# Alternating narrow and wide query tiles in a top-k attention, and a verdict sent by DMA instead of TensorE

## What is computed

```python
draft = einsum('bhqd,bhkd->bhqk', qr, kr) + causal          # rotary q and k
num_remain = max(min(Sq, 128), Sq - int(Sq * 0.9))          # 204 of 2048
_, idx = top_k(draft, num_remain)                           # all others masked
attn = softmax(einsum('bhqd,bhkd->bhqk', qr, kr) / sqrt(HD) + mask)
out = einsum('bhqk,bhkd->bhqd', attn, v) @ Wo.T
```

## Time and profile before

| | us |
|---|---|
| median of 3 runs | 4733.16 |
| lowest, highest | 4732.83, 4733.44 |
| the profiled execution, its own time | 4739.29 |
| its span | 4737.5 |
| busy in the span: PE, DVE, ACT, POOL | 3524.3, 3173.2, 2688.0, 2023.6 |

### The profile page before, as it was taken

How to read it: one execution, slowest core, us unless ns; L and a number is a source line. 1 busy time by engine, 2 the same in 40 slices (tenths; PEclk the granted TensorE clock), 3 DMA queues, 4 the chain that set the end, 5 groups by cost and what they waited for, 6 DMA issues and landing times. The chain is left out here.

```text
span 4737.5 us, 56552 instructions
## 1 busy us (share of the span) xinstructions
PE 3524.3 (74%) x16248; PEld 1649.4 (35%) x16248; DVE 3173.2 (67%) x6104; ACT 2688.0 (57%) x4577; POOL 2023.6 (43%) x5916
## 2 busy tenths in 40 slices
PE   5777775677868757787885678888567888857776
PEld 2333332233323323333332233333233333324443
DVE  2444444688988758888884888887488888822222
ACT  0111111688858757886885688887478888820000
POOL 1121211655535755554575554456565445620000
PEclk8777776688989878898997789989779999978887
DMA  2111111100001010000100100010010000011111
GB/s 97 42 52 43 51 40 44 34 11 11 9 6 21 16 30 12 11 9 7 21 16 19 24 11 9 9 21 14 19 26 11 9 9 11 15 72 53 54 40 40
DMA packets 221534, 124.04 MB, mean 26 GB/s; under 512 B 187940, under 2 KB 206628, under 8 KB 221092
## 3 DMA queue, kind: packets, MB, share of 16 engines
q1 hardware_dynamic: 221092, 119.36, 8.9%
HBM read 76.28 MB, written 42.99 MB: 25 GB/s over the span
## 5 line engine op out<-in xcount | busy, mean ns | idle before, releaser
L868 PE MATMUL banks<-pT,v_sb 128*65 128x512 f32 x2176 | 1186.3, 629 | 34.9 <-ACT oT L972 33.4
L957 ACT ACTIVATE pT<-banks 128x512 f32<-128x512 f32 x1088 | 637.7, 592 | 641.3 <-PE banks L840 634.9
L816 PE MATMUL banks<-k_sb,q_sb 128*128 128x512 bf16 (+3 forms) x1280 | 515.5, 403 | 388.5 <-DVE sc L1121 355.0
L1144 DVE MAX8 near<-keys 128x8 f32<-128x256 f32 (+14 forms) x480 | 653.4, 1361 | 16.5
L948 ACT ACTIVATE junk<-sc,t_all 128x256 fp8e4<-128x256 f32 (+14 forms) x480 | 599.2, 1249 | 31.9 <-DVE sc L1121 30.1
L948 ACT ACTIVATE junk<-sc,tiny 128x256 fp8e4<-128x256 f32 (+14 forms) x480 | 595.5, 1246 | 36.5 <-DVE sc L1129 36.2
L948 ACT ACTIVATE junk<-sc,tt 128x256 fp8e4<-128x256 f32 (+14 forms) x480 | 598.4, 1247 | 1.4 <-POOL tt L1013 0.8
L834 PE MATMUL banks<-q_sb,k_sb 128*128 128x512 bf16 x1088 | 447.0, 411 | 146.4 <-DVE fb L1298 124.7
L1121 DVE TENSOR_SCALAR_CACHE_REDUCE sc<-banks 128x1024 f32<-128x1024 f32 (+7 forms) x512 | 501.3, 980 | 52.1 <-PE banks L821 30.0
L1129 DVE TENSOR_SCALAR sc<-sc,tt 128x256 f32<-128x256 f32 (+14 forms) x480 | 360.5, 814 | 241.6 <-POOL tt L1034 241.5
L818 PE MATMUL banks<-k_sb,q_sb 96*128 96x512 bf16 (+3 forms) x1280 | 504.8, 404 | 0.0
(11 more groups left out here) (247 smaller groups left out, 5469.8 us busy)
## 6 DMA issues: line engine op xcount, KB each, us to landing
q_sb<-scratch_qk SPq DMA_DIRECT2D x896, 32.0 KB, 1.9
scratch_qk<-parts SPq DMA_DIRECT2D x16, 960.0 KB, 3.7
a_x<-in_x SPq DMA_DIRECT2D x16, 512.0 KB, 3.2
scratch_x<-a_x SPq DMA_DIRECT2D x16, 512.0 KB, 2.6
scratch_attn<-o_sb SPq DMA_DIRECT2D x128, 64.0 KB, 1.6
c_xn<-scratch_attn SPq DMA_DIRECT2D x16, 512.0 KB, 3.6
c_x<-scratch_x SPq DMA_DIRECT2D x16, 512.0 KB, 4.5
out<-c_x SPq DMA_DIRECT2D x16, 512.0 KB, 2.6
```

Of the source, the lines that this page charges most:

```text
L816: nc.tensor.matmul(r_slot(n)[:, j:j + wj], q_sb[:, p % QS, 0, h, :], k_sb[:, group[p] % 2, 0, col:col + wj], start=True, stop=False)
L868: nc.tensor.matmul(psum[0:VP, 6, :], v_sb[:, group[p] % 2, kb, :], pT[:, n % PTS, :], start=(kb == 0), stop=(kb == blocks[p] - 1)).then_in ...
L957: nc.scalar.activation(pT[:, tn % PTS, :], psum[:, 4 + n % 2, :], ACT.Exp, scale=SCALE)\
L1144: v.max(near[:, h, :], z).then_inc(sm["key"], 1)
```

## The change

First, the order of places. Within each group of heads the tiles now come as 0, 15, 1, 14, 2, 13, and so on to 7, 8. A narrow tile always stands beside a wide one, and the two tiles of a pair have 17 blocks together.

Second, the verdict. PE's `flags` and its wait for `bad` are gone, and so is the wait of `turn_back` for `flg`. Instead SP waits for `bad` and issues a transfer of it (128 rows of 4 bf16 numbers) into one partition, `verdict`; DVE waits for its landing and reads 512 numbers with one instruction. `bad` and `verdict` alternate between two buffers by the count of searched places. The list of small instructions in `fall_back` now finds the head from `verdict` on one partition.

```diff
-PLACE = [(g, i) for g in range(HKV) for i in (range(TILES) if g % 2 == 0 else range(TILES - 1, -1, -1))]
+PLACE = [(g, i) for g in range(HKV) for n in range(TILES // 2) for i in (n, TILES - 1 - n)]
...
+                def carry_verdict(p):
+                    sp.wait_ge(sm["bad"], chosen[p + 1])
+                    if p >= 2:
+                        sp.wait_ge(sm["go"], p - 1)
+                    sp.dma_start(verdict[0:1, chosen[p] % 2, :, :], bad[:, chosen[p] % 2, :]).then_inc(carried[chosen[p] % 2], 16)
+
...
                 for j in range(N + 2):
+                    if searching(j):
+                        carry_verdict(j)
                     if j >= 2:
                         store(j - 2)
...
-                    if chosen[min(p + 2, N)]:
-                        pe.wait_ge(sm["flg"], chosen[min(p + 2, N)])
...
-                def flags(p):
-                    pe.wait_ge(sm["bad"], chosen[p + 1])
-                    if p >= 2:
-                        pe.wait_ge(sm["norm"], p - 1)
-                    nc.tensor.matmul(psum[:, 7, FLAGS:FLAGS + REP], b.ones16[:, :], bad[:, p % 2, :],
-                                     start=True, stop=True).then_inc(sm["flagged"], 1)
...
-                    gp.tensor_tensor(bad[:, p % 2, :], c, far, ALU.add).then_inc(sm["bad"], 1)
+                    if chosen[p] >= 2:
+                        pool.wait_ge(carried[chosen[p] % 2], 16 * (chosen[p] // 2))
+                    gp.tensor_tensor(bad[:, chosen[p] % 2, :], c, far, ALU.add).then_inc(sm["bad"], 1)
...
-                    dve.wait_ge(sm["flagged"], chosen[p + 1])
-                    v.tensor_scalar(heads_bad[:, :], psum[:, 7, FLAGS:FLAGS + REP], 0.0, None, ALU.add, ALU.max,
-                                    accum_out=flg[:, 0:1]).then_inc(sm["flg"], 1)
+                    dve.wait_ge(carried[chosen[p] % 2], 16 * (chosen[p] // 2 + 1))
+                    if chosen[p]:
+                        dve.wait_ge(sm["flg"], chosen[p])
+                    v.tensor_scalar(passed[:, :], verdict[:, chosen[p] % 2, :, :].rearrange("o q h -> o (q h)"), 0.0, None,
+                                    ALU.add, ALU.max, accum_out=flg[0:1, 0:1]).then_inc(sm["flg"], 1)
```

More of the change, by code:

```diff
@@ L632 @@
 R_AT = (0.06, 0.25, 0.42)
-FLAG_AT, NEXT_R_AT = 1.0, 0.75
+NEXT_R_AT = 0.75
 def phase_b(nc, b, dram):
@@ L716, in phase_b @@
         heads_bad = sb("heads_bad", [P, REP])
+        verdict = sb("verdict", [1, 2, P, REP], BF16)
+        passed = sb("passed", [1, P * REP], BF16)
         rec = sb("rec", [P, REP])
@@ L728, in phase_b @@
         psum = b.psum
-        sm = semaphores(nc, ctx, "fill rs evac sign t1 t2 df sel key dk bad flagged flg mask go st ex pv ot otr norm mf "
+        sm = semaphores(nc, ctx, "fill rs evac sign t1 t2 df sel key dk bad flg mask go st ex pv ot otr norm mf "
                         "vchain pchain", "b")
@@ L735, in phase_b @@
         written = [ctx.enter_context(nc.semaphore(f"b_written{n}")) for n in range(2)]
+        carried = [ctx.enter_context(nc.semaphore(f"b_carried{n}")) for n in range(2)]
         def r_slot(n):
@@ L901, in _ @@
                     seen, back = 0, not here(j - 2)
-                    held = None
                     for n in range(len(todo) + 1):
                         for kind, p, h in at[n]:
[L905 to L910, removed]
+                            scores(p, h)
                         if n == len(todo):
@@ L1174, in fall_back @@
                         dve.drain()
[L1175 to L1179, removed]
+                        then(v.tensor_reduce(heads_bad[0:1, :], verdict[:, chosen[p] % 2, :, :].rearrange("o q h -> o h q"),
+                                             AX.X, ALU.max))
+                        then(v.tensor_scalar(heads_bad[0:1, :], heads_bad[0:1, :], 0.0, None, ALU.is_gt))
+                        then(v.tensor_reduce(several[0:1, :], heads_bad[0:1, :], AX.X, ALU.add))
+                        then(v.tensor_tensor(heads_bad[0:1, :], heads_bad[0:1, :], b.steps[0:1, 0:REP], ALU.mult))
+                        then(v.tensor_reduce(c[0:1, :], heads_bad[0:1, :], AX.X, ALU.max))
+                        then(v.tensor_scalar(which[0:1, :], c[0:1, :], 0.5, None, ALU.subtract))
                         hb = dve.value_load(fbi[0:1, 7:8], min_val=0, max_val=REP - 1)
@@ L1218, in fall_back @@
                         then(v.tensor_reduce(c[0:QUAD, :], quads[0:QUAD, :], AX.X, ALU.max))
-                        then(v.tensor_scalar(several, several, 1.5, None, ALU.is_gt))
-                        then(v.tensor_tensor(c[0:QUAD, :], c[0:QUAD, :], several[0:QUAD, :], ALU.max))
+                        then(v.tensor_scalar(several[0:1, :], several[0:1, :], 1.5, None, ALU.is_gt))
+                        then(v.tensor_tensor(c[0:1, :], c[0:1, :], several[0:1, :], ALU.max))
                         still = dve.value_load(fb[0:1, 0:1].bitcast(I32), min_val=0, max_val=FLAG_BITS)
@@ L1298, in _ @@
                         v.memset(fb[:, 7:8], 0.0).then_inc(sm["go"], 1)
-        clear(nc, [*sm.values(), *kload, *vload, *qload, *written])
+        clear(nc, [*sm.values(), *kload, *vload, *qload, *written, *carried])
 def build(nc, x, out, dram):
```

7 lines of the change are left out of this document (1 added, 6 removed).

## The result

The changed kernel takes 5367.03 us (median of 4 runs, 5364.76 to 5367.63), against 4733.30 us before in the same session (4732.83 to 4734.15, 4 runs). The ratio is 1.1338, with a 95% interval of 1.1318 to 1.1357. The profiled execution took 5364.76 us, with a span of 5363.0 us. The forecast was 5320 us, inside 5100 to 5480 us.

A forecast was written before the change was run, and what follows sets the result against it. A dependency chain over two stages bounds the kernel, no longer shared by wide neighbours: eight groups of 482.6 us make 555 us more, with the ends 587 over 4739.3, 5326; less the profiled run's 6.1, 5320 us, range 5100 to 5480.

The forecast's parts named there:

- The chain: From `go` two places back to a tile's own `go`; each new pair pays its wide tile's whole chain, 51.5 to 69.2 us.
- A: From `go` of place j - 2 through its units to place j's first third count: 31.0 us for 16 units.
- the bound of 29.5 us: Time from `go` through 16 units to the third counts if PE started at full clock: 29.5 us.
- S: A tile's four third counts on ACT, up to `directions`: 8.0 us at tile 15 down to 5.1 at tile 8.
- R: From `directions` to `go` of the same tile: 31.7 us at tile 15 down to 24.5 at tile 8.
- The two chains at the groups' seam: Chains of tile 15 and tile 8, where one group meets the next: 60.1 and 51.5 us.
- The verdict: DVE waits 2.6 us for the transfer and reads 0.3 us longer: 2.9 us on every wide tile's chain.
- The narrow stage: The narrow tile rides along; its verdict lies beside the wide tile's units and costs nothing unless its stage is late.
- the sign to look for: In the trace after, DVE idle some 8 us or more ahead of `directions` in wide stages, released by ACT.
- The ends: About 20 us more at the start, waiting for tile 15, and 12 us at the end, draining tile 8.
- Evened load: Rival: the busiest engine's work bounds a stage, so mixing widths gives a faster kernel, 4400 us; chance 0.08.
- The case with a narrow stage that is late as well: Rival: late narrow stages delay the next wide stage, and the verdict is at its upper bound: 5530 us; chance 0.13.

The follow-up runs named there:

- four units less: Four attention blocks left out of every wide tile, output incomplete: changed kernel 5093.69 us from 5367.03, kernel before 4615.13 us from 4734.17.
- all three early: Changed kernel with scores, second counts and third counts all placed earlier in the engines' lists: 5463.28 us.
- by twos: Kernel before with only the new alternating order of tiles, the verdict still on TensorE: 5268.98 us, ratio 1.1131.
- by fours: Kernel before with tiles ordered two narrow, two wide (0, 1, 15, 14, ...), the verdict still on TensorE: 5116.63 us, ratio 1.0814.

## Why the prediction was right, point by point

**The chain.** It held. In 53 of the 63 wide tiles that have a chain, `directions` starts within 0.2 us of the last third count. That the chains add up to the phase says nothing by itself, since they run from mark to mark; the response to the cut units does. Before, a wide tile cost 67.9 / 2 = 34.0 us and a narrow one (3350.6 - 64 x 34.0) / 64 = 18.4 us, together 52.4; after, a pair costs 62.1 us. The difference, 9.7 us by 64, is 621 us; measured from first to last mark, between these two lines, it is 3947.3 - 3350.6 = 597 us (the first pair is short).

```profile
864.93 0.06 DVE L1295 MEMSET fb<- 128x1 f32 x1
```

```profile
4812.25 0.06 DVE L1295 MEMSET fb<- 128x1 f32 x1 [0.46 <-DVE mk L1256]
```

**Its terms.** A was taken at 31.0 us for 16 units and measured 29.0. That is near the bound of 29.5 us, but not for that bound's reason: the start was slow, as the forecast had it. PE had stood idle for 13.92 us, and its granted clock was 0.50, the lower of its two levels, over the first 4.80 us of the stage; the same matmul took 0.63 us there and 0.38 us later.

```profile
4404.73 0.63 PE L846 MATMUL banks<-q_sb,k_sb 99*128 99x512 bf16 x1 [13.92 <-DVE fb L1295]
...
4410.02 0.38 PE L846 MATMUL banks<-q_sb,k_sb 99*128 99x512 bf16 x1
```

What was priced too high is the rest: behind the last unit's matmuls stood a first count of 1.67 us in the stage of the earlier trace rows, and one of a narrow tile, 0.60 us, here, which the forecast did not price. The last exponential starts 0.86 us after the start of the last unit here and 2.13 us there; that is 1.3 of the 2.0 us. A at tile 8 was 26.0 us and not 21.9 (seventh group), for a unit less is worth less than 1.52 us: four units less gave 5.0 us. That the mean came out exact (25.7 us) is luck, two errors that cancel. S was right. R at tile 14 was 29.3 to 29.6 us where 30.6 stood. The R of tiles 13 to 9 do not follow by slope from the ends as the prediction says: by slope tile 10 gets 25.5 us and not 27.4, and the five together 4.0 us less for each group. Measured, R at tile 10 is 28.2 us in the seventh group and 25.9 in the eighth. The two chains at the groups' seam were mis-sized: tile 15 with 64.9 us (60.1 predicted), tile 8 with 60.8 us (51.5). In the stage of tile 7 DVE waits 11.9 us for the second update of tile 8, so that differences, masks and `go` of tile 7 all come late; the counts of tile 8 are done before tile 8's stage has begun on DVE, and `directions` follows 4.8 us later, behind the copy of tile 15's scores. I had priced the wider copy in R and not its place ahead of `directions`, and nothing for the second update. Group 7 of 8 took 490.6 us where 482.6 stood: the two chains at the seam 14.1 us more than predicted, the other six 6.1 us less. That the total came within 1% owes something to luck.

**The verdict.** Mis-sized: 2.9 us for each wide tile predicted, 98 / 64 = 1.5 us measured. The wait was 0.86 us at tile 14 and not 2.6, because the judge needed 4.3 us from the start of `dk` (4462.33 to 4466.59) and not 6.0. The read was 0.5 us longer, not 0.3. The transfer took 1.9 us from issue to landing, not 1.6. The Trainium skill (DMA: Bandwidth & Descriptors, Anatomy of one DMA) gives about 2.0 us as the fixed part of a transfer issued from GpSimd; this one is issued from SyncE and holds 1 KB, and its 1.9 us are near that figure. PE's wait for `bad` was priced at nothing, and no run shows a gain from its going: with the verdict alone moved, the kernel is 157 us slower.

**The narrow stage.** "Costs nothing, unless late" held for the time, not for the picture. I had expected its idle time to show as a long wait ahead of the wide stage's directions, 8 us or more. It was 5.64 us at tile 14 here and 3.2 in the seventh group; the rest of the slack lies in the narrow stage itself, split over waits for scores, second update and transfer. So the sign to look for was wrong, while the cost was right.

**The ends.** The first mark comes 864.93 - 848.0 = 16.9 us later (20 predicted), and the time behind the last one is 550.8 against 538.9 us, 11.9 us more (12 predicted).

**The rivals.** Evened load is out: DVE's share fell to 69%. The advice to interleave regimes whose busiest engine differs (the Trainium skill, Perfetto Trace Analysis, Optimization Strategy) does not carry here: 535 us more by twos, 382 by fours. The case with a narrow stage that is late as well (5530 us) did not come either: shortening the narrow stage gave nothing. Only at the seam is a narrow stage, that of tile 7, late enough to hold up the wide tile behind it, by some 4.7 us in most groups.

**What stays open.** No list that I tried beats the kernel before. Whether a fourth buffer of scores, which would let the third counts stand ahead of the wide units, would let wide places overlap in the new order was not tried.

## What to carry to other kernels

When engines with fixed lists pass a place on over several stages, ask which step of one place waits for the end of another, and how many places share that chain: neighbours of like size share it, a small tile between two large ones takes the sharing away and gives back only its own small work. A low busy share in some stages is no room for others, if each stage also holds the neighbours' steps. And a wait can be slack beside another engine's backlog: a narrow stage 3.6 us shorter (all three early) brought the wide tile's directions no earlier. Taking a wait away usually puts another in its place; cut work from a suspected term to learn what it is worth.

## What the runs showed of the hardware

POOL's small instructions lasted about as long as the DVE instruction beside them. Before, six of the seven instructions of tile 15's judge took 1.05 to 1.21 us beside differences of 1920 keys (1.15 us each) and masks of 2048 (1.22 us each), and the judge 7.3 us in all. Here, at tile 14, the first five take 0.22 to 0.33 us, four of them beside differences of 384 keys (0.35 us each), and the last two, beside masks of 1920 keys (1.16 us each), 1.15 and 1.05 us. This judge takes 4.0 us from its first instruction (4462.63 to 4466.59), and that of tile 14 before took 6.9 us. Which part the engines share is not seen in the trace.

Ahead of `go`'s MEMSET DVE stands idle for up to 3.4 us with no semaphore to wait for (20 times before, 24 times after, "issue" in the waits). The trace's DMA packets show what goes with it. In the kernel after, 20 of these waits are over 2 us, and in each of the 20 a packet on one of the queues that load instructions (q8, q14) starts 1.75 to 2.1 us ahead of the MEMSET; at the other 108 MEMSETs this is so 3 times. Before it is 15 of 15, and 3 of 113. So these waits go with the loading of instructions; that it is DVE's own list which is loaded is likely, but the trace does not name the engine of a packet. The 20 waits are 59 us together; they are in every kernel here and explain nothing of the change.
